# Weight quantization in eight pieces over all slots, and reciprocals of row sums taken on reshaped rows that travel by transfer

## What is computed

```python
probs = jax.nn.softmax(scores.astype(jnp.float32), axis=-1)          # 16 heads, 1024 x 1024 each
ctx = jnp.einsum('bhqk,bhkd->bhqd', probs, v)
p_probs = jax.nn.softmax(p_scores.astype(jnp.float32), axis=-1)      # pattern heads
p_ctx = jnp.einsum('bhqk,bhkd->bhqd', p_probs, pv)
x = x + _layernorm(gates[..., 0:1] * main_out + gates[..., 1:2] * pattern_out)
...
amax = jnp.max(jnp.abs(wb), axis=1, keepdims=True)                   # blocks of 32 along K
scales = jnp.exp2(jnp.floor(jnp.log2(jnp.maximum(amax, 1e-30))) - 2.0)
idx = jnp.digitize(jnp.abs(wb / scales), FP4_MIDS)                   # seven thresholds
w = jnp.sign(wb) * FP4_GRID[idx] * scales                            # up (256x1024) and down (1024x256)
x = x + _layernorm(gelu(layernorm(x) @ w_up + up_bias) @ w_down + down_bias)
```

## Time and profile before

| | us |
|---|---|
| median of 3 runs (912.53 to 915.03) | 913.05 |
| the profiled execution | 913.16 |
| its span, first to last instruction | 911.4 |
| PE busy | 806.1 (88%) |
| DVE busy | 654.3 (72%) |
| POOL busy | 426.4 (47%) |
| ACT busy | 398.4 (44%) |
| TensorE's granted clock, mean | 0.959 of full speed |

### The profile page before, as it was taken

The page is one execution under the profiler, slowest core; times in us unless marked ns, Lnnn a source line. Parts: engine busy times, 40 slices in busy tenths (PEclk is TensorE's granted clock), DMA queues, the critical chain, the costliest instruction groups (busy, mean ns, idle before and its releaser), DMA issues. The chain is left out here.

```text
span 911.4 us, 12720 instructions
## 1 busy us (share of the span) xinstructions
PE 806.1 (88%) x4964; PEld 464.4 (51%) x4964; DVE 654.3 (72%) x768; ACT 398.4 (44%) x499; POOL 426.4 (47%) x255
## 2 busy tenths in 40 slices
PE   6868999998999899989998999999899969549975
PEld 5644555554545445545554554545445434138854
DVE  4836746747675778577757767675779999998656
ACT  4422354554455455545554555455445435200321
POOL 1343048438554665565566438554655444300232
PEclk9987999999999999999999999999999999869978
DMA  9476460042004200610240042004210710001001
GB/s 271 193 218 200 99 120 15 1 94 36 24 1 105 36 24 16 113 35 1 60 81 24 1 94 47 24 1 89 40 65 1 272 40 1 0 1 47 0 1 46
DMA packets 79615, 57.75 MB, mean 63 GB/s; under 512 B 53122, under 2 KB 62660, under 8 KB 79300
## 3 DMA queue, kind: packets, MB, share of 16 engines
q1 hardware_dynamic: 79556, 56.95, 24.5%
HBM read 33.63 MB, written 14.81 MB: 53 GB/s over the span
## 5 line engine op out<-in xcount | busy, mean ns | idle before, releaser
L859 POOL TENSOR_TENSOR acc<-acc,em 128x1024 f32<-128x1024 f32 x96 | 232.1, 2417 | 101.8 <-ACT em L917 101.8
L1010 DVE TENSOR_REDUCE m2p<-xb 128x2 f32<-128x1024 f32 x128 | 155.1, 1215 | 73.0 <-PE xb L1171 72.9
L1018 DVE TENSOR_REDUCE m<-xb 128x2 f32<-128x1024 f32 x128 | 155.4, 1217 | 58.6 <-PE xb L1171 57.3
L908 ACT ACTIVATE ep<-xb 128x1024 f32<-128x1024 f32 x128 | 131.2, 1025 | 117.0 <-PE xb L1171 117.0
L917 ACT ACTIVATE em<-xb 128x1024 f32<-128x1024 f32 x128 | 131.2, 1025 | 107.9 <-PE xb L1171 100.2
L1206 PE MATMUL pvm<-em,cpair 128*64 128x512 f32 x512 | 138.8, 621 | 0.0
L822 POOL TENSOR_TENSOR rot<-rot,sin 128x512 f32<-128x512 f32 x32 | 41.0, 1280 | 105.5 <-DMA rot<-raw 105.1
L1171 PEld LDWEIGHTS xb<-pq,pk 49*128 49x128 f32 x256 | 23.9, 184 | 100.9 <-issue 75.5
L859 POOL TENSOR_TENSOR acc<-em 128x1024 f32<-128x1024 f32 x16 | 38.7, 2420 | 63.1 <-PE xb L1314 55.0
L1217 PE MATMUL pvp<-ep,vp 128*32 128x512 f32 x512 | 68.2, 605 | 0.0
L1171 PE MATMUL xb<-pq,pk 49*128 49x512 f32 x256 | 64.3, 499 | 0.0
(11 more groups left out here) (272 smaller groups left out, 1387.6 us busy)
## 6 DMA issues: line engine op xcount, KB each, us to landing
rot<-raw SPq DMA_DIRECT2D x128, 64.0 KB, 2.0
pk<-spqk_d SPq DMA_DIRECT2D x48, 128.0 KB, 4.2
pq<-spqk_d SPq DMA_DIRECT2D x48, 64.0 KB, 2.3
ctx_d<-ctxr SPq DMA_DIRECT2D x12, 256.0 KB, 2.3
wraw<-wst_d SPq DMA_DIRECT2D x7, 384.0 KB, 5.4
em<-in_o_w SPq DMA_DIRECT2D x1, 2048.0 KB, 7.9
vp<-vp_d SPq DMA_DIRECT2D x8, 256.0 KB, 4.5
wqn<-in_q_b_w SPq DMA_DIRECT2D x1, 1536.0 KB, 10.7
```

The costliest lines, as they stand in the source:

```text
L859: pool.tensor_tensor(acc[:, :, :], before, em[:, j:j + 2, :], ALU.add).then_inc(added, 1)
L908: act.activation(ep[:, j:j + 2, :], src[:, :, :], ACT.Exp, scale=PAT_SCALE).then_inc(ep_ready, 1)
L1010: dve.tensor_reduce(m2p[:, t, 2 * tp:2 * tp + 2, kt], src[:, :, :], AX, ALU.max).then_inc(x_dve, 1)
L1018: dve.tensor_reduce(m2[:, q, t, :, kt], src[:, :, :], AX, ALU.max).then_inc(x_dve, 1)
```

## The change

**Quantization** is in eight pieces of 128 x 512, one in each of slots 1 to 8. A piece takes 20 steps of one instruction. `Q_STEP` says how many are done at each step of the slots 1 to 7; in slot 8 it is three a step until the piece is done. Each piece is loaded at the start of its slot (`load_natural`), stored to memory in the next (`store_ffn`), and the eight come back in slot 8 (`load_ffn`; the last in `load_last`). The buffers of the quantizer are now `work`, 128 x 2 x 1024, whose bytes are also those of `ctx67` (the first pieces used `cos`, `sin` and the `qm` tensors before).

**Reciprocals.** The row of `sums` of one head (512 values on one partition) is sent by transfer to 64 partitions of 8 values (`gather`, into `rs`), DVE takes the reciprocal of `rs` in one instruction of 128 x 8, the result is stored to memory and read back onto 64 partitions for each head (`spread`). The same for the pattern heads with `prs`, 128 x 16, four rows. The shuffle and all twelve quarter reciprocals of a slot are gone. The second half's reciprocal is at step 3, its division at step 6, the pattern division at step 7 (of the same slot in which its sums are ready, where it was steps 13 to 15), the first half's at steps 11 and 14.

**SP** has per slot 20 more transfers: one load and one store of a weight piece, four for `rs`, four for `prs`, six for spreading `rs`, of which two go to memory, and five for spreading `prs`, one of them to memory - and it waits for each store to land before it reads it back, and for DVE before each store. `DIRECT` goes from 12 to 14, so that two more halves pass through memory.

The core of the diff:

```diff
+Q_STEP = [1, 1, 3, 1, 1, 1, 1, 0, 0, 0, 1, 1, 1, 2, 3, 3]
...
-        DIRECT = 2 * NP - 4
+        DIRECT = 2 * NP - 2
...
+            def gather(n):
+                v, i = n // 2 + 1 + n % 2, n % 2
+                x_emptied(sp, v, ("S", i))
+                for h in range(2):
+                    sp.dma_start(rs[64 * h:64 * h + 64, :], sums[64 * h:64 * h + 1, :].rearrange(
+                        "o (p c) -> o p c", p=64)).then_inc(sum_in, 16)
+
+            def spread(n):
+                sp.wait_ge(rec_done, n + 1)
+                sp.dma_start(d["rec"][n].rearrange("h (p c) -> (h p) c", p=64), rs[:, :]).then_inc(rec_stored, 16)
+                sp.wait_ge(rec_stored, 16 * (n + 1))
+                for h in range(2):
+                    sp.dma_start(sums[64 * h:64 * h + 64, :], d["rec"][n, h:h + 1, :].broadcast_to((64, HALF))
+                                 ).then_inc(rec_in, 16)
...
+            def load_last():
+                store_ffn(7)
+                sp.wait_ge(ctx_stored, 16 * DIRECT)
+                for n in range(DIRECT - 2, DIRECT):
+                    half = half_of(n % 2)
+                    sp.dma_start(context_tile(g, n // 2)[:, half], d["ctx"][n // 2, :, half]).then_inc(ctx_back, 16)
+                load_ffn(7)
...
-                    for j in {2: (0, 1), 3: (2,), 4: (3,)}.get(s, ()):
-                        main_reciprocal(v, 1, j)
-                if 1 <= v <= NP and 10 <= s < 14:
-                    main_reciprocal(v, 0, s - 10)
-                late = {13: (0,), 14: (1, 2), 15: (3,)} if v <= NP else {5: (0, 1, 2, 3)}
...
+                    if s == 3:
+                        main_reciprocal(2 * (v - 2) + 1)
+                        pattern_reciprocal(v - 2)
+                    if s == 6:
+                        main_division(2 * (v - 2) + 1)
+                    if s == 7:
+                        pattern_division(v - 2)
+                if 1 <= v <= NP:
+                    if s == 11:
+                        main_reciprocal(2 * (v - 1))
+                    if s == 14:
+                        main_division(2 * (v - 1))
...
-                return (3 if s < 7 else 4) if v == NP else 6
...
+                    if 1 <= v <= NP:
+                        q_end = min(q_step + (Q_STEP[s] if v < NP else 3), QUANTIZE)
+                        for step in range(q_step, q_end):
+                            quantize(v - 1, step)
+                        q_step = q_end
```

More of the change, by code:

```diff
@@ L550, in attention @@
         prec = sb("prec", [P, HALF])
-        amax = sb("amax", [P, 32])
-        inv = sb("inv", [P, 32])
+        rs = sb("rs", [P, 2 * HALF // P])
+        prs = sb("prs", [P, 4 * HALF // P])
+        amax = sb("amax", [P, HALF // 32])
+        inv = sb("inv", [P, HALF // 32])
         wraw = sb("wraw", [P, 6, P])
@@ L565, in attention @@
         vo_out = [ctxr, sums, pvr, prec]
-        natural = [g["cos"], g["sin"]]
-        code, absolute, sign = (g[n + "_f"][:, :] for n in ("qm0h", "qm0l", "qm1"))
+        natural, sign, absolute, code = (g["work_f"][:, i // 2, i % 2 * HALF:(i % 2 + 1) * HALF] for i in range(4))
+        quantized = g["work"][:, 1, HALF:S]
         neg_in = [sem(f"neg_in{i}") for i in range(2)]
@@ L612, in attention @@
         vo_stored = sem("vo_stored")
-        ffn_in = [sem(f"ffn_in{i}") for i in range(2)]
-        transposed = sem("transposed")
+        nat_in = sem("nat_in")
+        ffn_stored = sem("ffn_stored")
         q_own = sem("q_own")
@@ new lines, in spread, with gather_pattern @@
+            def spread(n):
[5 more added lines that the diff above has]
+                                 ).then_inc(rec_in, 16)
+            def gather_pattern(it):
+                sp.wait_ge(pat_out, it + 1)
+                for hh in range(4):
+                    row = 32 * hh + PD
+                    sp.dma_start(prs[32 * hh:32 * hh + 32, :], pvr[row:row + 1, :].rearrange(
+                        "o (p c) -> o p c", p=32)).then_inc(psum_in, 16)
@@ new lines, in spread_pattern @@
+            def spread_pattern(it):
+                sp.wait_ge(prec_done, it + 1)
+                sp.dma_start(d["prec"][it].rearrange("h (p c) -> (h p) c", p=32), prs[:, :]).then_inc(prec_stored, 16)
+                if it:
+                    sp.wait_ge(pat_ready, it)
+                    sp.wait_ge(pat_stored, 16 * min(it, PDIRECT))
+                else:
+                    sp.wait_ge(vo_stored, 64)
+                sp.wait_ge(prec_stored, 16 * (it + 1))
+                for hh in range(4):
+                    sp.dma_start(prec[32 * hh:32 * hh + 32, :], d["prec"][it, hh:hh + 1, :].broadcast_to((32, HALF))
+                                 ).then_inc(prec_in, 16)
@@ new lines, in main_division, with pattern_reciprocal @@
+            def main_division(n):
+                dve.wait_ge(rec_in, 32 * (n + 1))
+                dve.wait_ge(ctx_out, n + 1)
+                to = ctxr[:, :]
+                if n >= DIRECT:
+                    to = context_tile(g, n // 2)[:, half_of(n % 2)]
+                    dve.wait_ge(q_own, 8 * QUANTIZE)
+                    dve.wait_ge(ffn_stored, 16 * 8)
+                dve.tensor_tensor(to, ctxr[:, :], sums[:, :], ALU.mult).then_inc(ctx_ready, 1)
+            def pattern_reciprocal(it):
+                dve.wait_ge(psum_in, 64 * (it + 1))
+                dve.reciprocal(prs[:, :], prs[:, :]).then_inc(prec_done, 1)
```

185 lines of the change are left out of this document (94 added, 91 removed).

## The result

The changed kernel takes 935.46 us (median of 4 runs, 931.3 to 937.7) against 912.79 (4 runs, 912.1 to 915.0): 1.0239 times as long, 95% interval 1.0199 to 1.0279. The forecast was 920.5 with a range of 897 to 940: the sign is right and the time lies in the range, but the loss is 22.7 us where 7.5 were forecast. The profiled execution took 935.39 us with a span of 933.6, so 22.2 us more span than before.

A forecast was written before the change was run, and what follows sets the result against it. PE was taken to set the pace in slots 2 to 7, DVE in slot 8 and the tail. Six slots +36.0, slot 1 +2.5, slot 8 -6.3, tail -24.9: +7.3 on 913.16, 920.5 us, range 897 to 940.

The forecast's parts named there:

- Tail: After the last slot: projection follows the last `pvp` without PE's 22.1 us wait, and the low clock goes; -24.9 us.
- Step 5: Slots 2 to 7: division and a reciprocal leave step 4, so PE's 2.19 us stall shrinks; -1.3 us a slot.
- Step 7: Slots 2 to 7: division and second instruction wait for POOL, delaying the `m2p` PE needs; +3.7 us a slot.
- Rival (a): At step 7 the division runs at once and only the second instruction waits; 905.6 us in all, chance 0.22.
- First tile M: Steps 14 and 15: DVE's waits for POOL delay the next slot's first tile M; +2.3 us a slot.
- Steps 2 and 3: Slots 2 to 7: gathers land before DVE asks for them at step 3; nothing lost.
- rival (c): Late gathers: `prs` lands late, DVE's step 3 instruction falls behind an add; 2.4 us more a slot, 935 us, chance 0.17.
- Clock: Slots 2 to 7: about 1.1 drops to 1.2 GHz a slot instead of a third; +1.3 us a slot.
- Slot 1: No division from a slot before; step 7 +1.0, step 2 +0.9, clock +0.6; +2.5 us.
- Slot 8: PE's idle time and half-clock stretches go, some stall, clock drop and quantizer waits come back; -6.3 us, bounds -12.8 and 0.
- Rival (d): Tail stays long because slot 8's loads or the last half's transfer chain end late; +10, 930 us, chance 0.08.
- The balance of DVE's load: DVE's work per slot: 12 us out, 10.6 us in; by load alone even.

The follow-up runs named there:

- experiments 5: Changed kernel with quantizer table 6,1,1,1,1,0,0,0,0,0,1,1,1,2,0,5, number 13's division at step 7, its store before the epilogue's loads, first piece loaded at end of slot 0: 885.03 us.
- 6: Changed kernel with step 6's quantizer instruction at step 10, step 14's three at step 15, number 13's store first, first piece loaded at end of slot 0: 873.52 us.
- 7: Kernel of experiments 5 with each slot's piece loaded ahead of the stack loads and the weight load: 871.72 us.
- 11: Kernel of 6 with each slot's piece loaded ahead of the stacks as well: 872.78 us.
- experiment 4: Changed kernel with the three quantizing instructions of step 14 moved to step 15: 907.94 us, median of nine.
- experiment 10: Changed kernel with the spread quantization, but the reciprocals on DVE as before, and number 13's store ahead of the epilogue's loads: 932.3 us.
- kernel 3: Changed kernel with the one quantizing instruction of step 6 moved to step 10: 911.58 us.

## Why the prediction missed the size

- **Tail, -24.9: measured -25.4.** Right in both parts. The projections follow at once, the last division of the pattern ends under them.
- **Step 5, -1.3: measured -2.1.** The single instruction was forecast to wait out part of an addition. It met POOL's `rc` in its place (599.30, 1.28 us) and took 1.38 us, so nearly the whole stall went, the lower bound of this term.
- **Step 7, +3.7: measured 3.5**, by the order of events that was forecast: `rc`, the division, the addition, the second instruction, in the rows above. (The step itself grew by 4.7 us, with the clock drop behind the stall.) Rival (a), the division first, did not occur.
- **First tile M, +2.3: measured 2.2.** Right, again by the sequence forecast: the waits at 562.48 and 565.36 are the two named.
- **Steps 2 and 3.** The gathers landed in 1.7 and 1.8 us (medians of `rs` and `prs`), near the floor taken, and in time; rival (c) did not occur. Step 3 lost 0.3 us in slot 6 and at most 0.9, in slot 7. The pieces of 32 and 64 B did not make them slow, so the rule on transfers under 512 B that the prediction quotes from the Trainium skill, "DMA: Bandwidth & Descriptors", changed nothing here.
- **Clock, +1.3 a slot: the failed step in the loop.** I counted 1.1 drops a slot; there were two in slots 3 to 7, one after each stall, at 1.5 us: 3 us against some 0.5 before, so +2.5. Step 5 gave part of that back, and slots 2 to 7 came to +37.9 where +36.0 stood in the sum.
- **Slot 1, +2.5: measured +5.7.** The step costed its instructions and not its load. The transposition waited 4.7 us for it, and PE 2.8 with one stretch at half clock behind it. Loaded at the end of slot 0, step 2 takes 4.3 to 5.2 us in place of 8.7 and the slot 82.4 to 85.1 in place of 86.3 (experiments 5, 6, 7 and 11).
- **Slot 8, -6.3: measured +3.1. This is the step that failed, 9.4 of the 15 us missed.** The terms that it had add up nearly right: with the store in its place slot 8 is 65.0 us against the 66 forecast. What was missing is a wait. The prediction followed number 13 to its place in memory and counted 29 loads and 7.4 MB, and did not ask who waits for its store, nor behind what SyncE issues it. Rival (d) had the right cause, slot 8's loads, with the wrong victim: it put the loss in the tail.
- **The balance of DVE's load.** "By load alone it is even" was short: DVE is busy 58.4 us with short additions, 2 more than the kernel before. It mattered as little as was said: 2.0 us over six slots.

Sum of the misses: slot 8 9.4, slot 1 3.2, slots 2 to 7 1.9, the start of the loop 0.7, epilogue 0.3, tail -0.5. That is 15.0, the distance between +7.3 and the +22.2 of the profiled times but for rounding. That 935.5 us lies inside the range of 897 to 940 is luck: it is above 931, the upper bound of the forecast's own terms, and the room above stood for rivals (c) and (d), neither of which occurred.

The mechanism stands on more than argument now. The waits, by the prediction's reading of the earlier trace rows, are those of DVE for POOL: with the additions shortened and nothing else touched, the quantizer's instruction fell from 1.821 to 0.720 us and the loss of the loop with it. The Trainium skill, "SBUF — State Buffer", on the ports that DVE and GpSimd share under an exclusive lock, is what the prediction drew on, and the traces agree with it: the waiting two-input instructions end 0.54 and 0.56 us after POOL's.

## What to carry to other kernels

In this kernel, spreading work over the loop paid once its place in each step was chosen by what it stands ahead of: elementwise DVE work beside a busy POOL belongs behind the reductions that free a bank, never two in a row ahead of one, and its size does not matter. For every buffer that a change sends through memory, name who overwrites it next and what is queued ahead of its store; for every load that a change adds, name what stands behind the instruction that waits for it. And price a recurring stall by its time plus the clock drop behind it.

## What the runs showed of the chip that I had not expected

- The stalls of 3.5 to 4.0 us in the loops were each followed by a stretch at 1.2 GHz, of 3.4 us but for one of 6.7 (experiment 4, slot 7). Of two stalls of 3.39 us in experiment 10 one was followed by 3.4 us of it (312.95) and one by none (687.29). The stalls of 2.2 us were followed by one only sometimes: in the kernel before in slots 2 and 3 and not in slots 4 to 7, whose clock is 1.00, in kernel 3 in slot 5 and not in slot 6. What decides between them stays open.
- A one-input DVE instruction on 128 x 16 numbers waits for POOL as long as one on 128 x 512: 2.25 us, 0.17 alone. What is left after POOL's end does shrink with the work: in the changed kernel 0.54 to 0.56 us for two inputs on 128 x 512, 0.27 to 0.29 for one, 0.02 to 0.04 for one on 128 x 16. Reciprocals and reductions that began beside POOL took no longer than usual (`rs` 0.19 us, `m` 1.22, the reduction to `amax` 0.68).
- A store of 256 KB issued behind 29 loads landed in 9.2 us and ahead of them in 2.2; a gather issued behind them at 806.7 was waited for until 814.8, where the median of these gathers is 1.7 us.
- The best of these kernels, with the whole change kept and only placed otherwise, takes 871.7 us: 4.5% less than the kernel before, where the change as it came was 2.4% slower.
